# A planned transformer kernel on one core: the first unit worked off by groups of features, its first stacks loaded early, and the planner's numbers retuned

## The chip, the cores and the metric

The kernel runs on 1 core of one Trainium2 chip. The metric is the device time of one execution in microseconds (us); lower is better. Every engine (PE is the matrix engine, ACT ScalarE, DVE VectorE, POOL GpSimd, SP the engine that here only issues DMAs) works through its own instructions in the order written, and waits on semaphores for the others.

## The reference: what is computed

Eight batches of 1024 tokens with 256 features, float32, through two layers. Each layer is a transformer block with adaptive layer normalisation (shift, scale and gate from a conditioning vector `c` through `silu(c) @ wmod`):

```
h = layernorm(x) * (1 + scale1) + shift1
x = x + gate1 * attention(h)          # 16 heads of 16, causal softmax
h = layernorm(x) * (1 + scale2) + shift2
x = x + gate2 * ffn(h)
```

Layer 0 has attention with a linear bias over positions and a feed-forward part with token mixing, a sigmoid gate and a squared ReLU; layer 1 has rotary embedding on queries and keys and a linear feed-forward part whose weight is a base matrix plus a low-rank product.

## The kernel before

Work is cut into 16 **units**, one for each batch and layer, in the order (0,0), (1,0), (0,1), (2,0), (1,1) and so on, so that a batch's two layers are two units apart. A unit has these kinds of items:

- *pre*: `ln` (layer normalisation: statistics on DVE, 4 steps of a chain on DVE, 14 on POOL, then `xn` on ACT), `turned` (transposes on PE), `qk` (8 turns: w = 0 for the queries and 1 for the keys, ft = one of two groups of 128 features, tb = one of two blocks of 512 tokens), `hi` on ACT and `split` on POOL (queries and keys as a float16 pair), `parts_save` (SP writes the pairs to DRAM), `value`.
- `stack_load` (SP reads one of four groups g of 4 heads back from DRAM into `stack_q` and `stack_k`, which hold one unit). Group 0 and 1 come from features ft = 0, groups 2 and 3 from ft = 1.
- `max` (L1634): 18 steps for each group, a first pass of scores whose row maxima DVE takes (L1419, L1421); then `join`, `rows` (L1643) and four small DMAs (L1037) that put the maxima into the stack.
- `score` (L1656) with ACT's exponential (L1208), `mask` on POOL (L1087), `context` (L1675), `save` and `norm`.
- *post*: `proj`, a second `ln`, the feed-forward part and the addition to x.

The order on every engine comes from one list. `plan` (L415) is a greedy planner in Python: at each step it takes, from the queues `score`, `context`, `max`, `pre` and `post`, the item with the lowest `price`, by a model of the engines with written-down costs (`Model`), waits (`SEEN`, `DMA_NS`) and pulls (`PULL`, `AHEAD`, `PHASES`, `FEED_WAIT`). The pre and post queues are kept in order. `with_start` adds what is done once: loads, the modulations `mods` (both layers' matrices `wmod`), the low-rank product and gates `once`, and `spill`. A stack group of unit u+1 can be loaded only when unit u's scores of that group are done.

One line matters below, in `Model.other`, the cost of a step of the chain (n = 0 is the aggregation on DVE):

```
self.ready["ln"] = self.ready["factors"] = self.run(engine, begin, 75 * (item[6] - item[5]) if n == 0 else 77, 110)
```

The first matrix product of the modulations (L1540), the gates (L1548), transposes (L1690), `qk` (L1580) and `value` (L1707) are the lines of PE at the start.

## Time and profile before

| what | value |
|---|---|
| median of 3 runs | 2705.45 us (2704.71 to 2705.87) |
| the profiled execution's own time | 2702.86 us |
| its span in the trace | 2701.1 us |
| PE busy | 2432.1 us, 90% |
| DVE busy | 2127.8 us, 79% |
| ACT busy | 1701.9 us, 63% |
| POOL busy | 1025.6 us, 38% |
| mean granted clock of PE | 0.968 of full speed |

Busy time is the union of an engine's instructions. PE at 90% leaves some 269 us in which it does nothing. The 1.8 us between span and time lie outside the trace.

### The profile page before, as it was taken

Reading aid. Unit: us, or ns where it says so; the run is one execution under the profiler, and the core shown is the slowest. Engines: PE = TensorE matmul, PEld = TensorE weight load, DVE = VectorE, ACT = ScalarE, POOL = GpSimd, SP = SyncE. Lnnn points to the kernel's source line nnn. Section 1 sums busy time; section 2 is a strip of 40 time slices with the busy share of each in tenths; the row PEclk is TensorE's granted clock in tenths of the full one; section 3 lists DMA queues with packets and bytes.
Section 4 is the critical chain, followed back from the end, with each engine's and each line's share of the span. In section 5 each row is a group of like instructions: output and inputs, shape, how many; then the busy total and the mean of one; then the engine's idle time right before and its main releaser. Section 6 shows DMA issues by size and latency. Waiting matters only on the chain. (4 is left out here: it accounts for less than half of the span.)

```text
span 2701.1 us, 56435 instructions
## 1 busy us (share of the span) xinstructions
PE 2432.1 (90%) x18968; PEld 1023.9 (38%) x18968; DVE 2127.8 (79%) x6588; ACT 1701.9 (63%) x3458; POOL 1025.6 (38%) x1558
## 2 busy tenths in 40 slices
PE   7798888999999999999999999999999999898586
PEld 4323434324334343443434343343434434344223
DVE  3898738898887988879887888879888798862972
ACT  3476574576765667666676677666677666665164
POOL 4222452245332544236243453325342363326222
PEclk9999999999999999999999999999999999999798
DMA  6511134113322222322312133222223123002300
GB/s 219 166 58 35 38 109 119 47 44 103 105 81 75 79 88 89 92 72 83 116 61 83 51 102 105 83 81 72 91 88 102 60 83 109 21 31 74 97 2 16
DMA packets 142400, 218.38 MB, mean 81 GB/s; under 512 B 21190, under 2 KB 62556, under 8 KB 142052
## 3 DMA queue, kind: packets, MB, share of 16 engines
q1 hardware_dynamic: 142120, 214.77, 25.9%
q8 instruction: 160, 2.62, 0.4%
q14 instruction: 120, 0.98, 0.1%
HBM read 137.87 MB, written 77.89 MB: 80 GB/s over the span
## 5 line engine op out<-in xcount | busy, mean ns | idle before, releaser
L1208 ACT ACTIVATE probs<-big 128x512 f32<-128x512 f32 (+2 forms) x2560 | 1218.9, 573 | 457.1 <-PE big L1656 451.5
L1421 DVE CUSTOM_DVE_ANT_0 big<-big,mask 128x128 f32<-128x128 f32 (+3 forms) x2048 | 940.0, 518 | 157.3 <-PE big L1634 155.0
L1656 PE MATMUL big<-stack_q,stack_k 64*128 64x512 f16 (+3 forms) x6144 | 684.6, 330 | 69.6 <-DVE mx L1421 27.0
L1419 DVE TENSOR_REDUCE mx<-big 128x1 f32<-128x512 f32 x1024 | 644.0, 679 | 119.2 <-PE big L1634 115.1
L1675 PE MATMUL ctx_ps<-probs,v_ones 128*17 128x512 f32 (+3 forms) x6144 | 645.3, 501 | 28.2 <-POOL probs L1087 26.6
L1087 POOL TENSOR_SCALAR_AFFINE_SELECT probs<-probs 128x512 f32<-128x512 f32 x512 | 332.5, 660 | 591.1 <-ACT probs L1208 590.9
L1634 PE MATMUL big<-stack_k,stack_q 64*128 64x512 f16 (+3 forms) x3072 | 434.9, 332 | 74.7 <-DVE mx L1421 39.5
L1656 PEld LDWEIGHTS big<-stack_q,stack_k 64*128 64x128 f16 x6144 | 222.5, 94 | 668.9 <-issue 470.9
L1634 PEld LDWEIGHTS big<-stack_k,stack_q 64*128 64x128 f16 x3072 | 136.3, 94 | 410.8 <-issue 254.3
L1421 DVE DVE_READ_ACCUMULATOR2_ANT mx<- 128x1 f32 x2048 | 282.8, 138 | 0.0
L1580 PE MATMUL big<-hT,w_qkv 128*128 128x512 f32 x512 | 266.4, 629 | 1.4 <-DVE mx L1421 0.5
L1180 POOL TENSOR_TENSOR region<-region 128x512 f16<-128x512 f32 x128 | 146.1, 1158 | 214.0 <-ACT region L1250 214.0
L1118 POOL TENSOR_TENSOR ctx_n<-ctx_b 128x256 f32<-128x256 f32 x128 | 83.0, 649 | 374.1 <-DVE ctx_b L1454 374.1
L1675 PEld LDWEIGHTS ctx_ps<-probs,v_ones 128*17 128x17 f32 x6144 | 109.8, 96 | 266.5 <-issue 190.2
L1257 ACT ACTIVATE xn<-x_res,nmr,rstd 128x256 f32<-128x256 f32 x256 | 129.5, 587 | 88.9 <-POOL nmr L1097 88.9
L1234 ACT ACTIVATE region<-big 128x512 f32<-128x512 f32 x128 | 76.5, 597 | 163.8 <-PE big L1580 163.8
L1451 DVE STREAM_TRANSPOSE ctx_b<-ctx_u 128x512 f32<-128x512 f32 x128 | 90.0, 703 | 77.9 <-ACT ctx_u L1218 77.9
L1707 PE MATMUL big<-w_qkv,hT 128*128 128x128 f32 x1024 | 143.0, 287 | 0.6 <-ACT region L1234 0.2
L1707 PEld LDWEIGHTS big<-w_qkv,hT 128*128 128x128 f32 x1024 | 123.6, 193 | 26.0 <-issue 15.8
L1591 PE MATMUL big<-w_out,ctxT 128*128 128x256 f32 x512 | 117.6, 386 | 8.5 <-DVE ctxT L1457 4.6
L1591 PE MATMUL big<-w_ffn,region 128*128 128x256 f32 x512 | 120.6, 390 | 3.9 <-DVE region L1485 3.7
L1690 PE MATMUL big<-ident,xn 128*128 128x128 f32 x512 | 78.6, 311 | 44.7 <-ACT xn L1257 42.9
(94 smaller groups left out, 1923.3 us busy)
## 6 DMA issues: line engine op xcount, KB each, us to landing
image<-region SPq DMA_DIRECT2D x192, 256.0 KB
stack_q<-image SPq DMA_DIRECT2D x64, 512.0 KB, 3.7
stack_k<-image SPq DMA_DIRECT2D x64, 512.0 KB, 4.5
lo_dram<-region SPq DMA_DIRECT2D x64, 256.0 KB
w_qkv<-wqkv SPq DMA_DIRECT2D x16, 768.0 KB, 4.9
x_res<-x SPq DMA_DIRECT2D x32, 256.0 KB, 2.9
stack_q<-lo_dram SPq DMA_DIRECT2D x128, 64.0 KB, 3.8
stack_k<-lo_dram SPq DMA_DIRECT2D x128, 64.0 KB, 4.5
```

The costliest lines, as they stand in the source:

```text
L1087: g.affine_select(out=diag, in_=diag, compare_op=ALU.is_ge, fill=0.0, base=0, pattern=[[0, GH], [1, P]], channel_multiplier=-1).then_inc(m ...
L1180: g.tensor_tensor(lo, own, hi, ALU.subtract).then_inc(split_done, 1)
L1208: s.activation(probs[:, n % HELD, heads, q0:], big[:, at.slot(turn), 0:len(pairs) * width] .rearrange("p (h q) -> p h q", h=len(pairs)), A ...
L1257: ins = s.activation(xn[:, t, :], x_res[:, batch % STREAMS, t, :], ACT.Identity, scale=rstd[:, t:t + 1], bias=nmr[:, t:t + 1])
L1419: last = v.reduce_max(to, held, AX)
L1421: last = v.tensor_tensor_reduce(out=held, in0=held, in1=mask[:, BANK - width:], scale=1.0, scalar=3.0 * NEG, op0=ALU.add, op1=ALU.max, acc ...
L1580: last = te.matmul(big[:, at.slot(), :], w[:, c, ft * P:(ft + 1) * P], rhs[:, c, tb * BANK:(tb + 1) * BANK], start=(c == 0), stop=(c == FC ...
L1591: last = te.matmul(big[:, at.slot(), t * D:(t + 1) * D], lhs[:, c, (n * 2 + t) * P:(n * 2 + t + 1) * P], w[:, c, :], start=(c == 0), stop= ...
L1634: last = te.matmul(big[:, at.max_bank(parity)[0], col:col + width], stack_q[rows, 0, g * PAIR_N + pair, qt * P:(qt + 1) * P], stack_k[rows ...
L1656: last = te.matmul(big[:, at.slot(at.turn() + parity), j * width:(j + 1) * width], stack_k[rows, c, g * PAIR_N + pair, kt * P:(kt + 1) * P ...
L1675: last = te.matmul(ctx_ps[32 * h:32 * h + DH + 1, q0:], v_ones[:, (2 * unit + g // 2) % V_HALVES, kt, (g % 2) * GH + h, :], probs[:, n % H ...
L1707: last = te.matmul(big[:, at.slot(), j * P:(j + 1) * P], h_all[:, c, t * P:(t + 1) * P], w_qkv[:, 2, c, half * P:(half + 1) * P], start=(c ...
```

## The change

It has four parts. (1) Unit 0's pre part gets an order of its own, `first_sequence`: both halves of the layer normalisation ahead of the first transposes, then queries and keys of ft = 0 for both blocks, their save, then ft = 1 and the values, and their save. (2) The saves of ft = 0 have a semaphore of their own, `early_saved`; stack groups 0 and 1 are loaded behind them, ahead of the saves of ft = 1, and groups 2 and 3 after those. No `max` is planned before the last `value` of unit 0. (3) Of the work done once, the modulations of layer 0 are cut in two (the half for the first normalisation stays ahead, the other half and the gates go behind `qk`), one wmod matrix gets another place in SBUF, two of the four loads of fixed rows and the x of batch 2 go behind the weights, and the memset of `stack_k` is cut in four. (4) The planner's numbers: a chain step on POOL is 200 ns and 85 ns to be seen, where it was 77 and 110; `SEEN`, `DMA_NS`, `FEED_WAIT` and `PHASES` have other values.

```diff
+def first_sequence():
+
+    first, second = layernorm_items(0, 0, 0, NT // 2), layernorm_items(0, 0, NT // 2, NT)
+    out = first + second[:-NT // 2] + turned(0, 0, 0) + second[-NT // 2:]
+    for ft in range(FC):
+        for tb in range(2):
+            out += turned(0, 0, 1) if (ft, tb) == (0, 1) else []
+            out += [(kind, 0, w, ft, tb) for w in range(2) for kind in ("qk", "hi", "split")]
+        out += [("value", 0, half, n) for half in range(2) for n in range(2)] if ft else []
+        out += [("parts_save", 0, w, ft) for w in range(2)]
+    return out + [("pre_loads", 1)]
...
-SEEN, DMA_NS = 326.2839, 466.9094
+SEEN, DMA_NS = 315.9617, 421.9575
...
+FIRST_FEED, FEED_WAIT = {"max": 216.0, "score": 430.0}, 160.9967
...
-                self.ready["ln"] = self.ready["factors"] = self.run(engine, begin, 75 * (item[6] - item[5]) if n == 0 else 77, 110)
+                self.ready["ln"] = self.ready["factors"] = self.run(engine, begin, 75 * (item[6] - item[5]) if n == 0 else 77 if engine == "DVE" else 200,
+                                                                              110 if engine == "DVE" else 85)
...
+        if kind == "parts_save" and item[2:] == (0, 1):
+            return ("stack_load", 0, 1) not in seen
...
-                if ("stack", *item[1:3]) not in model.ready:
+                if ("stack", *item[1:3]) not in model.ready or ("value", 0, 1, 1) not in seen:
...
-    after = {("stack_load", 0, 0): [("spill", 0), ("post_loads", 0)]}
+    after = {("pre_loads", 1): [("spill", 0), ("post_loads", 0), ("fixed_rows", 1)] + [("x_load", 2, n) for n in range(4)]}
...
+                    if not unit:
+                        sp.wait_ge(early_saved, 16 * SAVE_DMAS)
+                    if unit or g >= NG // 2:
+                        sp.wait_ge(parts_saved, at.now("parts_save", 0, 16 * SAVE_DMAS))
...
-            g.memset(stack_k[:, 1], 0.0).then_inc(stacks_clear, 1)
+            for g_ in range(NG):
+                g.memset(stack_k[:, 1, g_ * PAIR_N:(g_ + 1) * PAIR_N], 0.0).then_inc(stacks_clear, 1)
```

The planner's order changes with it everywhere. First, PE behind the last values of unit 0 (L1707 before, L1753 in the change; the row of `ident,xn` is unit 1's 16 transposes, `hT,w_qkv` is unit 1's `qk`, `stack_k,stack_q` is `max`). Before:

```order
L1707 MATMUL big<-w_qkv,hT 128x128 x16
L1690 MATMUL big<-ident,xn 128x128 x16
L1580 MATMUL big<-hT,w_qkv 128x512 x2
L1634 MATMUL big<-stack_k,stack_q 128x128 x2
L1634 MATMUL big<-stack_k,stack_q 128x384 x2
L1634 MATMUL big<-stack_k,stack_q 128x256 x4
L1580 MATMUL big<-hT,w_qkv 128x512 x2
```

PE at the same place in the change:

```order
L1753 MATMUL big<-w_qkv,hT 128x128 x16
L1736 MATMUL big<-ident,xn 128x128 x16
L1680 MATMUL big<-stack_k,stack_q 128x128 x2
L1680 MATMUL big<-stack_k,stack_q 128x384 x2
L1680 MATMUL big<-stack_k,stack_q 128x256 x4
L1680 MATMUL big<-stack_k,stack_q 128x512 x4
L1680 MATMUL big<-stack_k,stack_q 128x128 x2
```

The first `max` still stands behind unit 1's transposes; the `qk` that stood between is now behind the whole of group 0.

Second, PE in the change where the first `score` stands (`stack_q,stack_k`, L1702; it was L1656). Before, 33 steps of `max`, 8 turns of `qk` and 3 of `value` stand ahead of it; here 44, 7 and none beyond those of unit 0:

```order
L1627 MATMUL big<-hT,w_qkv 128x512
L1680 MATMUL big<-stack_k,stack_q 128x512 x4
L1627 MATMUL big<-hT,w_qkv 128x512
L1680 MATMUL big<-stack_k,stack_q 128x512 x2
L1627 MATMUL big<-hT,w_qkv 128x512
L1702 MATMUL big<-stack_q,stack_k 128x512 x8
```

What moved is the first `score` against `max`: 11 steps further back.

Third, SP from unit 0's first save on, in the change (`image<-region` and `lo_dram<-region` are saves; before, all four pairs of them stood ahead of the first load of `stack_q`):

```order
L1044 DMA image<-region 8x16x1024 [waits split_done]
L1044 DMA image<-region 8x16x1024 x2
L1046 DMA lo_dram<-region 128x1024
L1044 DMA image<-region 8x16x1024 [waits split_done]
L1044 DMA image<-region 8x16x1024 x2
L1046 DMA lo_dram<-region 128x1024
L1061 DMA stack_q<-image 128x2x1024 [waits early_saved,rows_in]
...
L1044 DMA image<-region 8x16x1024 [waits split_done,stacked_1,stacked_0]
```

The saves of ft = 1 now wait until the first two stack groups have landed.

## Rows read from the trace of the kernel before

**Rows 1.** The page: the head, busy time and instructions of PE and DVE.

```profile
PE 2432.1 (90%) x18968; PEld 1023.9 (38%) x18968; DVE 2127.8 (79%) x6588; ACT 1701.9 (63%) x3458; POOL 1025.6 (38%) x1558
```

**Rows 2.** Stretches: length, busy us by engine (x count), PEclk, DMA share, GB/s.

```profile
80.00:104.00 24.00, 16.74 (x68) 4.68 (x67) 23.67 (x82) 6.13 (x10) 14.80 (x13) 0.98 0.77 215
121.60:238.50 116.90, 106.39 (x1026) 32.88 (x1025) 111.09 (x359) 86.23 (x182) 27.14 (x44) 1.00 0.20 61
238.50:420.00 181.50, 156.20 (x1103) 68.02 (x1103) 106.33 (x316) 113.88 (x227) 82.10 (x121) 0.96 0.22 66
2540.00:2580.00 40.00, 26.35 (x195) 8.49 (x195) 36.57 (x123) 14.12 (x32) 8.75 (x12) 0.66 0.15 44
```

**Rows 3.** PE's timeline: start, length, what, idle before and its releaser.

```profile
12.15 6.97 PE L1540 MATMUL big<-ctx_b,region 128*128 128x8 f32 x32 [12.15 <-DMA region<-wmod]
19.05 3.58 PE L1548 MATMUL ctx_ps<-region,ctx_b 128*8 128x256 f32 x8
22.56 1.97 PE L1690 MATMUL big<-ident,xn 128*128 128x128 f32 x8
...
59.16 3.84 PE L1707 MATMUL big<-w_qkv,hT 128*128 128x128 f32 x32
72.04 3.67 PE L1690 MATMUL big<-ident,xn 128*128 128x128 f32 x16 [9.04 <-ACT xn L1257]
...
77.73 0.61 PE L1634 MATMUL big<-stack_k,stack_q 64*128 64x128 f16 x8
...
121.63 1.12 PE L1656 MATMUL big<-stack_q,stack_k 64*128 64x512 f16 x8
...
238.46 7.14 PE L1591 MATMUL big<-w_out,ctxT 128*128 128x256 f32 x32 [0.78 <-DVE ctxT L1457]
```

**Rows 4.** PE's waits from 600 to 2400 us: us, times, longest.

```profile
PE big L1656 <- DVE mx L1421: 18.4, 38, 1.9
...
PE big L1690 <- ACT xn L1257: 6.5, 6, 1.8
```

**Rows 5.** ACT's timeline: the first normalised tiles.

```profile
17.08 2.07 ACT L1257 ACTIVATE xn<-x_res,nmr,rstd 128x256 f32<-128x256 f32 x4 [13.42 <-POOL nmr L1097]
```

**Rows 6.** SP's timeline: the first save, the first stack load.

```profile
40.16 2.03 SPq L1008 DMA_DIRECT2D image<-region  x3
...
65.76 0.37 SPq L1023 DMA_DIRECT2D stack_q<-image  x1
```

**Rows 7.** DVE's timeline: the first step of `max`, and the first `join`.

```profile
78.19 0.30 DVE L1421 CUSTOM_DVE_ANT_0 big<-big,mask 128x128 f32<-128x128 f32 x1 [13.20 <-PE big L1634]
...
102.39 0.19 DVE L1430 TENSOR_TENSOR mxc<-mx 128x32 f32<-128x32 f32 x1 [0.33 <-DVE mx L1421]
```

**Rows 8.** The page's costliest groups: busy us, mean ns | idle before.

```profile
L1656 PE MATMUL big<-stack_q,stack_k 64*128 64x512 f16 (+3 forms) x6144 | 684.6, 330 | 69.6 <-DVE mx L1421 27.0
L1675 PE MATMUL ctx_ps<-probs,v_ones 128*17 128x512 f32 (+3 forms) x6144 | 645.3, 501 | 28.2 <-POOL probs L1087 26.6
L1634 PE MATMUL big<-stack_k,stack_q 64*128 64x512 f16 (+3 forms) x3072 | 434.9, 332 | 74.7 <-DVE mx L1421 39.5
```

**Rows 9.** PE's timeline: a `max` visit of four matmuls, one of two.

```profile
1007.09 0.61 PE L1634 MATMUL big<-stack_k,stack_q 64*128 64x512 f16 x4
1007.62 0.84 PE L1675 MATMUL ctx_ps<-probs,v_ones 128*17 128x384 f32 x8
...
1024.20 0.39 PE L1634 MATMUL big<-stack_k,stack_q 64*128 64x512 f16 x2 [0.37 <-DVE mx L1421]
1024.52 1.05 PE L1675 MATMUL ctx_ps<-probs,v_ones 128*17 128x512 f32 x8
```

**Rows 10.** Timelines near the end: saves, first load, DVE's additions; the last unit's transposes.

```profile
2478.27 2.27 SPq L1008 DMA_DIRECT2D image<-region  x3
...
2494.78 0.39 SPq L1023 DMA_DIRECT2D stack_q<-image  x1
...
2494.78 0.69 DVE L1464 TENSOR_TENSOR x_res<-x_res,big 128x512 f32<-128x512 f32 x1 [3.24 <-PE big L1591]
...
2425.66 3.68 PE L1690 MATMUL big<-ident,xn 128*128 128x128 f32 x16 [5.50 <-ACT xn L1257]
```

More of the change, by code:

```diff
@@ L159, with save_of, saved_early @@
 QK_LAGS = (0.0, 0.7758, 0.9862, 2.3391, 5.9576)
+def first_sequence():
[8 more added lines that the diff above has]
+    return out + [("pre_loads", 1)]
+def save_of(unit, g):
+    return [("parts_save", unit, w, *((g // 2,) if unit == 0 else ())) for w in range(2)]
+def saved_early(item):
+    return item[0] == "parts_save" and item[3:] == (0,)
 def pre_sequence(unit):
     layer = UNITS[unit][1]
+    if unit == 0:
+        return first_sequence()
     out = normed_and_turned(unit, 0)
@@ L292, in other_needs @@
         if kind == "parts_save":
-            return max(self.at(("split", *item[1:], ft, tb)) for ft in range(FC) for tb in range(2)), "SP"
+            return max(self.at(("split", *item[1:3], ft, tb)) for ft in item[3:] or range(FC) for tb in range(2)), "SP"
         if kind == "ln":
@@ L350, in other @@
             self.ready[kind, item[1]] = self.moved(self.run("SP", begin, 450), 768, 0.180)
+            if item[1] == 1:
+                self.ready["post_loads", 0] = self.moved(self.run("SP", begin, 2600), 2400, 0.180)
         elif kind == "parts_save":
-            self.ready[kind, item[1], item[2]] = self.moved(self.run("SP", begin, 3600), 2048, 0.180)
+            self.ready[item] = self.moved(self.run("SP", begin, 3600), 1024 if item[3:] else 2048, 0.180)
     def bank(self, end):
@@ L473, in barred @@
         if kind in ("scale", "bias"):
-            return (("post_loads", unit) if unit else ("stack_load", 0, 0)) not in seen or open_("pre", unit, "ln")
+            return (("post_loads", unit) if unit else ("pre_loads", 1)) not in seen or open_("pre", unit, "ln")
         return False
@@ L509, in follow @@
                 u, g = loads[0]
-                saved = model.at(("parts_save", u, 0), ("parts_save", u, 1))
-                if ("parts_save", u, 1) not in seen or (u and ("last", u - 1, g) not in seen) \
-                        or saved > max(now, model.free["SP"]) + EASE:
+                saved = model.at(*save_of(u, g))
+                if save_of(u, g)[1] not in seen or (u and ("last", u - 1, g) not in seen) \
+                        or (u, g // 2) != (0, 0) and saved > max(now, model.free["SP"]) + EASE:
                     break
@@ L656, in events @@
         e["turn"] = 2 if kind == "score" else 1
+    if kind == "parts_save" and item[3:]:
+        del e[kind]
+        if item[2]:
+            e["early_save" if saved_early(item) else kind] = 1
     if kind == "max":
@@ L1001, in step @@
                     own = qk_place(layer, w)[1]
-                    for ft in range(FC):
+                    saved = early_saved if saved_early(item) else parts_saved
+                    for ft in item[3:] or range(FC):
                         heads, half = slice(ft * HH, (ft + 1) * HH), slice(0, DH)
@@ L1532, in _, with modulations @@
             pe.wait_ge(consts_set, 3)
-            def modulations(l):
-                for k, part in enumerate((0, 3, 1, 4)):
+            def modulations(l, which):
+                for k in which:
+                    part = (0, 3, 1, 4)[k]
                     for fc in range(FC):
@@ L1557, in once @@
                     gates_of(1, small[0:B, 1, :])
-                    modulations(1).then_inc(once_mm, 1)
+                    modulations(1, range(4)).then_inc(once_mm, 1)
                     pe.wait_ge(once_v, 1)
```

62 lines of the change are left out of this document (34 added, 28 removed).

## The prediction

> **What bounds the kernel now.** I read the page first. PE is busy 2432 of 2701 us and DVE 2128 [rows 1], so on the average PE is the bound, with 269 us of idle time in which any gain must lie, beside what PE's own work costs. Then the busy time by stretches [rows 2]. It shows that the average hides three regimes. From 80 to 104 us DVE is busy 23.67 of 24.00 us: the row maxima of unit 0 fill it, and PE waits. From 121.6 to 238.5 us DVE still has 111.1 of 116.9 and PE 106.4. After 238.5 both fall (156.2 and 106.3 of 181.5): unit 2 needs unit 0's result, and the work that may be put between runs short. The timeline of PE [rows 3] dates the marks that matter here: the last value at 59.16, unit 1's transposes at 72.04, the first `max` at 77.73, the first `score` at 121.63, unit 0's first `proj` at 238.46. The list of PE's waits in the middle of the run [rows 4] shows which waits the retuned planner could remove: on DVE's maxima 18.4 us in one of its groups, on `xn` only 6.5 us in 1800.
>
> **The start of unit 0.** Before, the first transposes begin at 22.56 [rows 3], though their tiles are ready at 17.08 + 2.07 = 19.15 [rows 5]: PE still works on the modulations and gates. In the change half of the modulations (6.97 / 2 = 3.5 us) and the gates (3.58) stand behind `qk`, so the transposes can begin at about 19.2, 3.4 us earlier, and the second half's chain no longer waits on DVE behind the modulations, which may double it to 6.8. The moved work comes back later: 7.1 us at the clock it had, 3.5 if it runs at twice that. So the last value of unit 0 moves by between -3.3 and +3.7 us. I take -1.3, as PE is in steady work by then. Unit 1's statistics, chain and `xn` hang on DVE's `once` steps, which move with it; so its transposes begin at about 70.7 where they began at 72.04.
>
> **The early stacks.** The four saves and their landing took from 40.16 to 65.76, 25.6 us [rows 6]. Two of them take 12.8, and the first begins some 6 us earlier, when ft = 0 is done: about 34 + 13 = 47, and two stack groups have landed before 60. That is far ahead of before. But in the new order the first `max` stands on PE behind unit 1's 16 transposes, and these wait for `xn`, not for a stack. The early load therefore gives nothing of its own. What the order gives is that no `qk` turn stands between: before, 72.04 + 3.67 = 75.7 to 77.73, 2.0 us. DVE's first step moves from 78.19 [rows 7] to 78.2 - 1.3 - 2.0 = 74.9. Groups 2 and 3 come late (their saves wait for the first two stacks, their loads stand behind spill, weights, tails and x), at 95 to 100 by the same rates, and are needed after 36 steps of `max`, at about 123: hidden; without that cover each us late is lost on DVE.
>
> **The first scores.** A group of 18 steps took DVE 102.39 - 78.19 = 24.2 us [rows 7], 1.345 each. Before, 33 steps stand ahead of the first `score`: 44.4 us, and it began 43.4 after DVE's first step. In the change there are 44: 74.9 + 59.2 - 1.0 + 0.5 for the second `rows` = 133.6, where it was 121.63, **+12.0**. For PE this is a hole: in it stand 44 `max` and 7 `qk`, and nothing else. A cost for the clock comes on top. Where PE had as little to do, from 2540 to 2580, the granted clock was 0.66 and DVE was busy 91% against 99% from 80 to 104 [rows 2]; carried over 59 us that is at most 4.6 us, and 0 if the clock stays at 0.98; I take 2. So the first `score` comes 14 us late. The Trainium skill (TensorE: Matmul & The Clock Gate, "What's actually happening") says that the slow clock is the default and activity releases it; the low clock in that row agrees, and by the rule the whole hole could run at 1.2 GHz, which would make the term the 4.6 us above.
>
> From there to the first `proj` the same 86 scores have to be done. An item costs PE, from the busy time [rows 8] over 1280 scores, 768 contexts and 1152 `max` steps of the plan, 0.53, 0.84 and 0.38 us; a value turn 3.84 / 2 = 1.9 [rows 3], a `qk` turn 2.0. Into this stretch come 3 values, 1 `qk` and 1 context (8.5 us), out of it go 8 `max` (3.0): 106.4 + 5.5 = 111.9 us of PE's work. DVE's falls by 8 x 1.345 to 100. So PE is the bound, and the stretch takes 111.9 to 122.4 (with all the idle time it had), against 116.9. I take 4 us of idle: 115.9, -1. First `proj` of unit 0: **+13 us**, at about 251. Bounds +9.5 to +22. Nothing absorbs it: at `proj` both orders have done the same (86 scores), and unit 2 hangs on it.
>
> **Units 1 and 2.** PE idles 25 us between 238.5 and 420 [rows 2]. With the chain on POOL planned at its real length less of it is spent on `xn`; I take -3. Changes between the three kinds of tile on PE also fall: over the whole plan from 2128 to 2046, 33 of them in units 1 and 2 and 51 in units 5 to 12. A visit of its own costs 0.11 us: a `max` visit of four matmuls takes 1007.62 - 1007.09 = 0.53, one of two 0.32 [rows 9], so the second pair costs 0.21. That is -3 here (not all on the path): **-6** in all, between 0 and -10.
>
> **The steady middle.** 51 x 0.11 = -5.6, and of the 6.5 us of waits for `xn` [rows 4] I take 2: **-7.6**. The other waits depend on how the orders mesh. The work between a group's last `max` and its `rows`, and between a diagonal score and its context, is spread much as before, so I take 0, with 15 us either way (of 107 us of idle in that stretch a seventh).
>
> **The end.** Unit 15's stacks are loaded at 2494.78, after saves that began at 2478.27 [rows 10] and took as long. In the change these saves stand 5 scores and 3 contexts further ahead: 2.7 + 2.5 = 5.2 us gained. But `proj` of unit 14 is now mixed with the first `max`, so DVE's four additions of 0.69 fall into the stretch that DVE bounds: +2.8. Unit 15's transposes waited 5.50 us for `xn` [rows 10]; its chain begins with 5 more `max` at hand: -3. **-5.4**, between -9 and +4.
>
> **Sum.** +13 - 6 - 7.6 - 5.4 = -6.0. On the profiled execution's 2702.86 that is 2696.9; this lay 2.6 below the median, so against the runs 2699.5. I say 2698.
>
> **The rivals.**
> *The start is lost and not bought back.* The place is the stretch from the first `max` to the first `proj`. If the hole costs the +13 to +17, and the middle gives only its fewer changes (and these partly under waits, -3), the sum is +7 to +14: 2710 to 2719. For it: +13 comes from counted items and measured steps, the gains mostly from small terms. It decides once the later terms give less than 8 us. Against: the end's term has its own rows.
> *The middle meshes better.* The retuned pulls may also cut waits on DVE (18.4 us in one group alone [rows 4]) and on masks. 12 us off 107 gives 2686; with a PE-bound stretch after the hole as tight as its floor, 2680. For it: more PE work is left over in each unit, since `max` runs less far ahead. Against: the spacing of items shows no such thing.
> *The change does nothing.* The early stacks are hidden behind `xn`, and plans trade waits one for one: 2703 to 2708.
>
> **How the numbers follow.** The sum as worked out, 2690 to 2703: 0.38. Better mesh, 2675 to 2690: 0.24. Nothing, 2703 to 2710: 0.14. Loss, over 2710: 0.24. A measurement tells 0.2%, 5.4 us, so faster is under 2700: 0.24 and two thirds of 0.38, 0.48; slower 0.24; same 0.28. The range leaves out about 0.1 at either end: 2681 to 2715. The sum's own range is 2690 to 2703.
>
> **What the changed profile would show.** Unit 1's transposes at 70 to 71 with a wait on `xn`, the first `max` right behind them near 74.4; PE idle about 27 us and a lower granted clock from there to the first `score` near 134; first `proj` near 251; idle time between 600 and 2400 of about 107 us; the load of unit 15's first stack about 5 us sooner after its scores. A first `score` before 128, or a middle that is 15 us shorter or longer, would make the forecast wrong.

## The result and the profile after

The changed kernel takes **2728.73 us** (median of 4 runs, 2726.71 to 2735.23) where the kernel before took 2705.66 (4 runs beside them, 2704.71 to 2706.28). The ratio is 1.0086, 95% interval 1.0074 to 1.0098: 23 us slower. 2698 was predicted, faster by 7. The profiled execution has a span of 2727.1 us and a granted clock of 0.968, as before. On another chip the same kernel gave 2728.88 (5 runs).

The page of the changed kernel, PE's line, answers to [rows 1]:

```profile
PE 2425.3 (89%) x18968; PEld 1025.8 (38%) x18968; DVE 2128.9 (78%) x6590; ACT 1699.4 (62%) x3458; POOL 1028.0 (38%) x1561
```

PE is 6.8 us less busy over the run, near the 8.6 that was forecast for fewer changes of tile form; whether it is that is asked further down. But it is idle for 2727.1 - 2425.3 = 301.8 us where it was idle for 269.0. All of the loss is idle time, and more than all.

The windows of the changed kernel, with the columns of [rows 2] (the second and third rows are the stretches from the first `score` to the first `proj` and from there to 420):

```profile
80.00:104.00 24.00, 12.74 (x47) 3.39 (x45) 23.93 (x84) 0.00 (x0) 0.00 (x0) 0.50 0.82 258
...
136.40:254.00 117.60, 109.81 (x1068) 39.67 (x1067) 102.16 (x327) 89.06 (x188) 30.05 (x46) 1.00 0.27 80
254.00:420.00 166.00, 139.99 (x996) 63.89 (x998) 94.44 (x265) 104.92 (x208) 76.49 (x113) 0.95 0.18 57
2540.00:2580.00 40.00, 27.64 (x165) 13.84 (x169) 39.63 (x141) 12.35 (x24) 10.38 (x22) 0.79 0.05 15
```

From 80 to 104 us the hole is there that the prediction described: PE busy 12.74 of 24 us where it was 16.74, ACT not once, DVE busy 23.93 of 24, the clock granted at 0.50. PE's timeline of the changed kernel gives the marks that answer to [rows 3]:

```profile
12.00 3.56 PE L1585 MATMUL big<-ctx_b,probs 128*128 128x8 f32 x16 [12.00 <-DMA probs<-wmod]
...
19.18 1.11 PE L1736 MATMUL big<-ident,xn 128*128 128x128 f32 x4 [3.62 <-ACT xn L1297]
...
71.53 3.68 PE L1736 MATMUL big<-ident,xn 128*128 128x128 f32 x16 [10.41 <-ACT xn L1297]
75.14 1.46 PE L1680 MATMUL big<-stack_k,stack_q 64*128 64x128 f16 x10
...
124.87 0.40 PE L1689 MATMUL big<-ident,mxc 128*32 128x128 f32 x1 [4.34 <-DVE mxc L1473]
...
136.45 0.61 PE L1702 MATMUL big<-stack_q,stack_k 64*128 64x512 f16 x4
...
253.99 2.18 PE L1638 MATMUL big<-w_out,ctxT 128*128 128x256 f32 x9 [0.55 <-issue]
```

DVE's timeline in the hole: the first step of `max`, the `join` behind 18 steps, and the first step behind 36:

```profile
75.82 0.30 DVE L1464 CUSTOM_DVE_ANT_0 big<-big,mask 128x128 f32<-128x128 f32 x1 [11.65 <-PE big L1680]
...
99.73 0.19 DVE L1473 TENSOR_TENSOR mxc<-mx 128x32 f32<-128x32 f32 x1
...
127.58 0.30 DVE L1464 CUSTOM_DVE_ANT_0 big<-big,mask 128x128 f32<-128x128 f32 x1 [1.69 <-PE big L1680]
```

The first `max` is 2.6 us earlier than before, the first `score` 14.8 later, the first `proj` 15.5 later. SP's timeline, for [rows 6]: first save, first stack load, the save of ft = 1, the load of group 2:

```profile
36.39 2.02 SPq L1044 DMA_DIRECT2D image<-region  x3
...
50.14 0.38 SPq L1061 DMA_DIRECT2D stack_q<-image  x1
...
61.20 1.88 SPq L1044 DMA_DIRECT2D image<-region  x3
...
85.53 1.63 SPq L1061 DMA_DIRECT2D stack_q<-image  x1
```

The first stack load is issued 15.6 us earlier than before and 25 us ahead of its first user. PE's waits of the changed kernel from 600 to 2400 us answer to [rows 4]:

```profile
PE big L1680 <- DVE mx L1464: 21.6, 49, 2.3
PE big L1702 <- ACT probs L1247: 19.0, 51, 0.8
PE big L1702 <- DVE mx L1464: 15.2, 30, 1.7
PE ctx_ps L1721 <- POOL probs L1126: 11.6, 11, 1.6
PE big L1680 <- DVE mx L1462: 11.1, 21, 1.0
PE big L1680 <- ACT probs L1247: 9.5, 38, 1.8
PE big L1638 <- DVE region L1529: 8.5, 5, 2.8
```

and these rows of the same view of the kernel before, which [rows 4] leaves out:

```profile
PE ctx_ps L1675 <- POOL probs L1087: 16.4, 17, 2.2
PE big L1634 <- DVE mx L1421: 13.4, 47, 1.1
...
PE big L1656 <- ACT probs L1208: 9.1, 17, 0.7
...
PE big L1634 <- ACT probs L1208: 6.1, 20, 0.6
```

The waits for `xn` (6.5) are gone from these rows; 0.2 are left. In their place the `max` matmuls (L1680) wait 21.6 us for the maxima of L1464 where they waited 13.4 (then L1421), scores and `max` together wait 28.5 us for ACT where it was 15.2, and `proj`'s line waits 8.5 on `region` where it waited 0.5. Some waits fell: scores for L1464 from 18.4 to 15.2, contexts for POOL from 16.4 to 11.6. In all PE is idle 131.2 us of this window where it was idle 107.1.

To date a loss I read the last `score` of every unit off PE's timeline (unit u's is the matmul of L1702 with number 384(u + 1); the last line gives PE's last matmul). The first column is in us from the start; the others say how much later each kernel is (all traces are laid on each other at the first modulation, which moves them by up to 0.9 us). The column "again" is a second trace of the changed kernel, on another chip. The kernels of the last five columns are told of below.

```
 last score   before   changed   again   e7     e10    e17    e12     e8
 unit 0        228.5    +16.2    +16.8  +16.1   +2.1   +1.5    0.0   +0.9
 unit 1        417.4    +11.8    +11.9  +16.2   +2.3   +3.6   +1.9   +1.4
 unit 2        606.5    +14.1    +12.6  +17.7   +1.9   +4.3   +3.7   +1.6
 unit 3        752.5     +8.0     +6.4  +17.4   +1.6   -2.0   +3.6   +1.6
 unit 4        923.4    +18.9    +17.3  +18.0   +2.3   +8.9   +3.3   +1.4
 unit 5       1067.0     +9.4     +7.8  +18.1   +2.4   -0.6   +3.3   +1.4
 unit 7       1381.9    +13.5    +11.9  +18.1   +2.5   +7.3   +0.6   +1.0
 unit 9       1694.8    +18.8    +17.1  +18.2   +2.5  +15.0   +7.0   +2.8
 unit 11      2009.2    +21.4    +19.7  +18.7   +3.0  +18.7  +10.8   +1.4
 unit 12      2179.8    +32.2    +28.6  +17.5   +2.9  +26.3  +18.5   +1.5
 unit 13      2315.3    +39.4    +34.6  +18.3   +2.9  +32.9  +24.3   +3.8
 unit 15      2668.1    +24.5    +20.0  +18.8   +0.1  +18.4  +21.3  -11.1
 last matmul  2697.3    +26.1    +21.3  +19.2   +0.4  +19.7  +21.9  -10.6
```

So the changed kernel has three parts: 16 us lost by the first scores, 30 lost from unit 5 to unit 13 (27 in the second trace), 13 won at the end. Two cautions. Single traces differ: e8 and e12 have the order of before up to unit 13 and unit 5, and still stand off by up to 3.8 us there; the two traces of the changed kernel come to differ by 4.8. And the marks are not of equal work. At the last `score` of unit 5 the changed kernel has issued 76 matmuls of unit 6's `max` where the kernel before has issued 92, at that of unit 4 it is 90 against 92. So unit 5 flatters it: from unit 4 to unit 12 (82 against 92) it loses 13 us.

### The profile page after: what moved, and what is told of

Read it like the earlier page. It is cut to its first block and busy times, and to the rows that moved or that the text cites. A ratio compares the mean times of both kernels' runs of the same rounds, so it can differ in the third digit from the quotient of the medians.

```text
span 2727.1 us, 56456 instructions
## 1 busy us (share of the span) xinstructions
PE 2425.3 (89%) x18968; PEld 1025.8 (38%) x18968; DVE 2128.9 (78%) x6590; ACT 1699.4 (62%) x3458; POOL 1028.0 (38%) x1561
## 5 line engine op out<-in xcount | busy, mean ns | idle before, releaser
L1464 DVE CUSTOM_DVE_ANT_0 big<-big,mask 128x128 f32<-128x128 f32 (+3 forms) x2048 | 939.5, 520 | 205.3 <-PE big L1680 201.7
L1702 PE MATMUL big<-stack_q,stack_k 64*128 64x512 f16 (+3 forms) x6144 | 676.9, 327 | 68.7 <-ACT probs L1247 26.5
L1721 PE MATMUL ctx_ps<-probs,v_ones 128*17 128x512 f32 (+3 forms) x6144 | 638.1, 496 | 30.2 <-POOL probs L1126 21.5
L1680 PE MATMUL big<-stack_k,stack_q 64*128 64x512 f16 (+3 forms) x3072 | 445.4, 335 | 108.5 <-DVE mx L1464 49.5
L1702 PEld LDWEIGHTS big<-stack_q,stack_k 64*128 64x128 f16 x6144 | 223.2, 94 | 635.7 <-issue 444.6
L1680 PEld LDWEIGHTS big<-stack_k,stack_q 64*128 64x128 f16 x3072 | 139.2, 94 | 455.5 <-issue 231.5
L1464 DVE DVE_READ_ACCUMULATOR2_ANT mx<- 128x1 f32 x2048 | 285.0, 139 | 0.1
L1753 PE MATMUL big<-w_qkv,hT 128*128 128x128 f32 x1024 | 139.5, 286 | 0.2 <-DVE mx L1464 0.2
L1638 PE MATMUL big<-w_out,ctxT 128*128 128x256 f32 x512 | 123.7, 400 | 10.6 <-issue 5.3
L1753 PEld LDWEIGHTS big<-w_qkv,hT 128*128 128x128 f32 x1024 | 123.1, 194 | 23.3 <-issue 17.0
L1304 ACT ACTIVATE v_ones<-big 128x512 f32<-128x512 f32 x64 | 38.3, 598 | 142.2 <-PE big L1753 142.1
```

The costliest lines, as they stand in the source:

```text
L1464: last = v.tensor_tensor_reduce(out=held, in0=held, in1=mask[:, BANK - width:], scale=1.0, scalar=3.0 * NEG, op0=ALU.add, op1=ALU.max, acc ...
L1638: last = te.matmul(big[:, at.slot(), t * D:(t + 1) * D], lhs[:, c, (n * 2 + t) * P:(n * 2 + t + 1) * P], w[:, c, :], start=(c == 0), stop= ...
L1680: last = te.matmul(big[:, at.max_bank(parity)[0], col:col + width], stack_q[rows, 0, g * PAIR_N + pair, qt * P:(qt + 1) * P], stack_k[rows ...
L1702: last = te.matmul(big[:, at.slot(at.turn() + parity), j * width:(j + 1) * width], stack_k[rows, c, g * PAIR_N + pair, kt * P:(kt + 1) * P ...
L1721: last = te.matmul(ctx_ps[32 * h:32 * h + DH + 1, q0:], v_ones[:, (2 * unit + g // 2) % V_HALVES, kt, (g % 2) * GH + h, :], probs[:, n % H ...
L1753: last = te.matmul(big[:, at.slot(), j * P:(j + 1) * P], h_all[:, c, t * P:(t + 1) * P], w_qkv[:, 2, c, half * P:(half + 1) * P], start=(c ...
```

## The experiments

**Start, chain and numbers apart.** Taken roughly, the changed kernel is a new start (parts 1 to 3 of the change, which stay together here), a new cost of the chain on POOL, and new numbers (both in part 4). Each of these four kernels has some of them.

e2, the kernel before with the new numbers:

```diff
-SEEN, DMA_NS = 326.2839, 466.9094
+SEEN, DMA_NS = 315.9617, 421.9575
...
-FIRST_FEED, FEED_WAIT = {"max": 216.0, "score": 430.0}, 300.0000
+FIRST_FEED, FEED_WAIT = {"max": 216.0, "score": 430.0}, 160.9967
```

(and the new `PHASES`.) 

> Before, with only the new SEEN, DMA_NS, FEED_WAIT and PHASES. Start as before. If these numbers spoil the middle: 10 to 20 us over before, by a drift of 3 to 5 us for each pair of units. If the chain cost does: within 5 us of before.

Measured: 2728.92, ratio 1.0085 (1.0068 to 1.0102): 24 us over before, more than either case had.

e3, the kernel before with the chain's cost alone:

```diff
-... 77, 110)
+... 77 if engine == "DVE" else 200, 110 if engine == "DVE" else 85)
```

> Before, with only the chain step on POOL planned at 200 and 85 ns. The plan has 2046 changes of tile kind instead of 2128, as few as the changed kernel. If fewer changes and an honest chain are worth what the prediction gave them: 5 to 10 us under before. If the chain cost is what spoils the middle: 10 to 20 us over before, with the waits for xn gone and those on DVE and ACT grown.

Measured: **2781.54**, ratio 1.0283 (1.0268 to 1.0298). It has as many changes of tile form as the changed kernel, 2046, and is 53 us slower than that. Both expected ranges are missed: 10 to 20 us was the worse one, 76 came.

e4, the changed kernel with the chain's cost and all the numbers of before:

```diff
-SEEN, DMA_NS = 315.9617, 421.9575
+SEEN, DMA_NS = 326.2839, 466.9094
...
-... 77 if engine == "DVE" else 200, 110 if engine == "DVE" else 85)
+... 77, 110)
```

> The new start, with the chain cost and all planner numbers of before. Theory 1 (the loss has two separate parts: the hole ahead of the first score, and a middle that the new chain cost and numbers spoil): first proj of unit 0 about 15 us late as in the changed kernel, no drift behind it, so 5 to 15 us over before. Theory 2 (a late start tips the greedy order of the whole run): the middle drifts here too, 20 us or more over before.

Measured: **2781.85**, ratio 1.0282 (1.0267 to 1.0298). Its start is that of the changed kernel (last `score` of unit 0 at +16.0), and from unit 1 to 5 it falls back by 36 us more. That is theory 2's case, and more than its 20 us.

e5, the kernel before with the chain's cost and the new numbers:

```diff
-SEEN, DMA_NS = 326.2839, 466.9094
+SEEN, DMA_NS = 315.9617, 421.9575
...
-... 77, 110)
+... 77 if engine == "DVE" else 200, 110 if engine == "DVE" else 85)
```

> Chain cost and new numbers on the start of before. If the parts add up, the changed kernel less the 10 to 12 us that unit 1's last score is late: 2714 to 2720. If start and numbers only go wrong together: near before, 2700 to 2708.

Measured: 2717.04, ratio 1.0045 (1.003 to 1.006): inside the range of "if the parts add up". It adds up in this one place, the start against all the rest; the sums that follow do not add.

Over the kernel before, in us: start alone +77, chain alone +76, numbers alone +24, chain and numbers +12, all three +23. The parts do not add (chain and numbers would give 100, the start 12 or 77), and none of them is faster. Each part alone lets the planner write out a new order of 7286 items, and the order is what is timed. So to learn what a part costs, the order has to be held still.

**Orders cut and joined.** In the next kernels the order is a table. `ordered` gives the planner's items in that order, and `replay` plays them through the model, for it is the model that hands out the banks of PSUM. In the lines below `old` and `new` are the orders before and after, and `then(a, b)` is `a`, followed by what is not yet in it, in the order of `b`.

```diff
-PLAN = plan(MODEL)
+PLANNED = plan(MODEL)
+PLAN = ordered(PLANNED)
+MODEL = replay(PLAN)
```

e6, the new program and its start, then the old order:

```diff
-order = new
+order = then(new up to the first max, old)
```

> The changed program with its new start (feature groups, early saves and stack loads, mask fill in pieces), but from the first `max` on in the order of the kernel before, word for word: 33 `max` steps before the first `score`, not 44. Theory 1 (the late first `score` and the drift behind it are made by the order alone): first `max` near 75 us as in the changed kernel, first `score` at 119 to 122, and the whole at 2700 to 2707. Theory 2 (the new start costs by its own work: loads that share the queues, DVE operations beside the fill, a lower clock): first `score` near 130 or later and 2715 to 2720, although the order is the old one.

Measured: 2711.52 (8 runs), ratio 1.0021 (1.0011 to 1.0031). The time lies between the theories; the first `score` comes at 131.4, as theory 2 had it. Its PE timeline shows why:

```profile
72.72 3.38 PE L1971 MATMUL big<-ident,xn 128*128 128x128 f32 x16 [8.82 <-ACT xn L1532]
83.36 3.75 PE L1862 MATMUL big<-hT,w_qkv 128*128 128x512 f32 x4 [7.26 <-DMA w_qkv<-wqkv]
87.05 1.03 PE L1915 MATMUL big<-stack_k,stack_q 64*128 64x128 f16 x8
```

In the old order a `qk` of unit 1 stands ahead of the first `max`, and in the new program its weights land late, since SP issues their load behind the four saves (at 73.76). PE waits 7.26 us for them with the stacks long there. The line numbers are higher by the table of the order.

e7, the new order up to the first `proj`, the old one behind it:

```diff
-order = new
+order = then(new up to the first proj of unit 0, old)
```

> The changed kernel's start and its order up to the first `proj` of unit 0, and from there the order of the kernel before. Theory 1 (what is lost before the first `score` is lost for good, and the middle's own order adds the rest): the 12 to 16 us of the start stay and nothing is added, 2717 to 2721. Theory 2 (the changed middle is what repairs part of the lost start, as the last scores of units 1 to 4 suggest, and without it the loss grows): 2725 or more. Theory 3 (a middle that runs in the old order takes up a late start, because its engines wait anyway): under 2710.

Measured: 2722.23, ratio 1.0058 (1.0043 to 1.0073). That is 1.2 us beyond theory 1's range, and outside the other two. The column e7 above is the plainest of the study: +16.1 at unit 0 and +18.8 at unit 15. What is lost ahead of the first scores is not taken up anywhere in 2400 us of the old order.

e8, the old program and order, but the new order at the end:

```diff
-order = old
+order = then(old up to the last score of unit 13, new)
```

> The kernel before, start and all, up to the last `score` of unit 13, and what is left from there in the changed kernel's order. In the changed kernel the distance to before shrinks from 39 us at that point to 26 at the end. Theory 1 (the order of the last two units is better by itself): 13 us come off, 2690 to 2695. Theory 2 (the distance shrinks since work that had been put off in the middle of the changed order was done by then, or since other work had been done ahead): nothing comes off, 2703 to 2710.

Measured: **2691.80**, ratio 0.9948 (0.9934 to 0.9963): theory 1, and 14 us faster than the kernel before. The windows of before, then of e8, from 2400 to 2545:

```profile
2400.00:2545.00 145.00, 111.98 (x762) 51.69 (x760) 76.76 (x218) 70.60 (x143) 59.50 (x84) 0.87 0.30 91
```

```profile
2400.00:2545.00 145.00, 116.86 (x848) 52.04 (x840) 94.39 (x275) 78.54 (x159) 61.89 (x89) 0.92 0.28 84
```

DVE does 17.6 us more in the stretch. It is the row maxima of the last unit (118 matmuls of `max` on PE there, before 82): its first `max`, before and in e8, on PE's timelines:

```profile
2501.82 0.83 PE L1634 MATMUL big<-stack_k,stack_q 64*128 64x128 f16 x10 [1.33 <-DMA stack_k<-lo_dram]
```

```profile
2421.75 0.67 PE L1756 MATMUL big<-ident,xn 128*128 128x128 f32 x4 [0.20 <-ACT xn L1323]
...
2490.82 1.46 PE L1700 MATMUL big<-stack_k,stack_q 64*128 64x128 f16 x10 [5.07 <-DMA stack_k<-lo_dram]
```

11.0 us earlier, and the 5.50 us wait of unit 15's transposes for `xn` [rows 10] is 0.20. SP's first load of that unit's stacks in e8, which stood at 2494.78 [rows 10]:

```profile
2483.53 0.38 SPq L1089 DMA_DIRECT2D stack_q<-image  x1
```

e9, the kernel before with 2 ns on one number:

```diff
-SEEN, DMA_NS = 326.2839, 466.9094
+SEEN, DMA_NS = 328.2839, 466.9094
```

> The kernel before with one number of the planner moved by next to nothing, 2 ns in 326 (the time after which an engine is taken to see another's result). 1448 of the 7286 places of the order change, all behind place 492; it has 2105 changes of tile form for 2127. Theory 1 (the numbers of the kernel before were chosen for this one order, and any other order of the same planner is worse): 2715 to 2740, with the first 150 us as before. Theory 2 (the planner gives orders of equal worth when its numbers move a little, and what the change cost comes from its parts): 2700 to 2710.

Measured: **2720.37**, ratio 1.0055 (1.0038 to 1.0072). 2 ns in a planner's assumption, which say nothing of the chip, cost 14.4 us: theory 1.

e10, as e6 with six `max` ahead of unit 1's first `qk`:

```diff
-order = then(new up to the first max, old)
+order = then(new up to the first max + old's first 6 max, old)
```

> As the kernel with the new start and the old order, but the first 6 `max` steps stand ahead of unit 1's first projection, since in that kernel the first `max` came only at 87.5 us, behind a projection that waited to 83.4 for layer 1's weights. Still 33 `max` steps before the first `score`. Theory 1 (the new start is not slower in itself; what it lost in that kernel was this wait): first `max` near 75 us, first `score` at 119 to 122, and 2700 to 2707 in all. Theory 2 (the new start only moves the wait, since layer 1's weights come later in it): first `score` at 126 or later, and 2709 to 2713.

Measured: 2704.20 (10 runs), ratio 0.9998 (0.9989 to 1.0008). Its PE timeline, and its window from 80 to 104:

```profile
75.69 0.50 PE L1915 MATMUL big<-stack_k,stack_q 64*128 64x128 f16 x6
...
80.99 7.60 PE L1862 MATMUL big<-hT,w_qkv 128*128 128x512 f32 x12 [0.27 <-DMA w_qkv<-wqkv]
...
124.39 0.90 PE L1937 MATMUL big<-stack_q,stack_k 64*128 64x512 f16 x6
```

```profile
80.00:104.00 24.00, 19.64 (x64) 6.58 (x64) 19.28 (x59) 7.36 (x12) 14.42 (x13) 0.89 0.82 260
```

The time is as theory 1 has it. The mark is not: the first `score` comes at 124.4, 2 us beyond the upper bound, since DVE has only 19.28 us of work in these 24 where it had 23.67 [rows 2]. That is my own edit: the `qk` that the old order strings between the six moved `max` now stand in one row of twelve matmuls, and DVE has nothing to do for 4.54 us of them. Even so the new start costs nothing in front of the old order.

e11, as e10 with e8's end:

```diff
-order = then(new up to the first max + old's first 6 max, old)
+order = then(then(that, old) up to the last score of unit 13, new)
```

> The kernel of the run before this one, and from the last `score` of unit 13 on the changed kernel's order, which took 14.2 us off the kernel before. If what the stages lose and win adds up, it is 14 below the run before this one: 2686 to 2693. If the joins cost, or if the gain at the end belonged to one order ahead of it, 2695 to 2705.

Measured: 2694.15, ratio 0.9959 (0.9944 to 0.9974). It lies between the two ranges, 1.2 us over the first one's end. The gain over e10 is 10.0 us where e8 had 14.2; with 4 runs here and spreads of 4 and 8 us in the two kernels, these are hardly told apart.

e12, the changed order in the middle alone:

```diff
-order = old
+order = then(then(old up to the last score of unit 5, new) up to the last score of unit 12, old)
```

> The kernel before with the changed kernel's order in its middle alone: from the last `score` of unit 5 to that of unit 12; the rest as before. It has 2083 changes of tile form for 2127. In that stretch the changed kernel fell back by 22.9 us (9.2 to 32.1). Theory 1 (the order of the stretch makes it by itself, whatever came ahead): the last `score` of unit 12 is 18 to 26 us later than before, and the whole is 2722 to 2732. Theory 2 (the drift is an after-effect of the late start): 2703 to 2709. The prediction's own claim (fewer tile changes, the rest even) would give 2699 to 2702.

Measured: **2725.73**, ratio 1.008 (1.0065 to 1.0095). Theory 1: the middle by itself, behind an untouched start, costs 20 us. PE's waits there, before (1067 to 2180 us), five rows of thirteen, and e12 (1067 to 2202), six of thirteen:

```profile
PE big L1656 <- DVE mx L1421: 12.9, 26, 1.9
PE ctx_ps L1675 <- POOL probs L1087: 11.0, 10, 2.2
PE big L1634 <- DVE mx L1421: 6.5, 27, 0.4
PE big L1656 <- ACT probs L1208: 6.3, 12, 0.7
...
PE big L1634 <- DVE mx L1419: 3.1, 10, 0.6
```

```profile
PE big L1787 <- ACT probs L1339: 12.0, 30, 0.8
PE big L1765 <- DVE mx L1552: 11.4, 26, 2.2
PE ctx_ps L1806 <- POOL probs L1218: 9.6, 9, 1.6
PE big L1787 <- DVE mx L1552: 9.2, 10, 1.7
PE big L1765 <- DVE mx L1550: 7.9, 16, 0.9
...
PE big L1722 <- DVE region L1616: 4.5, 4, 1.7
```

At the last `score` of unit 12 e12 is 18.5 us late, of which 3.3 stood there at unit 5 already, under before's order. Between these two marks PE is idle 80.5 us where it was idle 63.2, and busy 2.1 us less. The thirteen rows sum to 57.0 before and to 71.9 in e12. The matmuls of `max` (L1634, now L1765) wait 19.3 us for DVE instead of 9.6, the scores for DVE 10.7 instead of 14.3; the scores wait 12.0 us for ACT instead of 6.3; `proj`'s line waits 4.5 on `region` for 0.2, and 4.0 in which the profile shows no wait are new. No engine got more work. Why just these waits grew was not tested: that `max` matmuls stand closer together than DVE empties their banks would explain the largest part of it.

e13, units 2 and 3 by e2's order, and e8's end:

```diff
-order = then(old up to the last score of unit 13, new)
+order = old to unit 1, e2's to unit 3, old to unit 13, then new
```

> The kernel before and its start, with units 2 and 3 in the order of the kernel that had the new numbers alone (where they took 8.4 us less, from last `score` to last `score`), and with the changed kernel's order from the last `score` of unit 13. If stages add up, 2691.8 - 8.4 = 2683, so 2681 to 2686. If the 8 us were only borrowed (other work put off, to be done in unit 4), 2690 to 2694.

Measured: 2705.66 (10 runs), ratio 1.0001 (0.9992 to 1.0011): 14 us worse than e8, and outside both ranges. At the last `score` of unit 3 it is 5.0 us ahead of before, at that of unit 5 14.9 behind. Unit 3's first `proj` comes 14.7 us later than before, although its last `score` was early: the lead was borrowed. What had been put off can be counted in the traces. At the last `score` of unit 3, before has issued 92 matmuls of unit 4's `max`, e13 only 72; at the first `proj` both have issued 112. The contexts left over are the same (32 matmuls). So 20 more matmuls of `max`, 7 or 8 steps, stand ahead of that `proj`; at 1.345 us a step on DVE [rows 7] I estimate 10 of the nearly 20 us from them. The rest is open.

**What puts the first score late.** The planner's model sends every transfer through one queue. The change adds 2400 KB to it (`post_loads` 0, behind `pre_loads` 1), and the 16 KB of the first `rows` stand behind them. Without that one entry the planner puts 36 `max` ahead of the first `score`, not 44.

e14, that entry out, for the order up to the first `proj`:

```diff
-order = new
+order = then(new without the 2400 KB, up to the first proj of unit 0, new)
```

> The changed kernel, with its order up to the first `proj` of unit 0 from a planner whose model doesn't put the 2400 KB of `post_loads` 0 into its one queue of transfers; from there the changed kernel's own order. 36 `max` steps stand before the first `score`, not 44. Theory 1 (this entry is what puts the first `score` late, and the late start is worth its 11 us in the changed kernel too): first `score` at 75.8 + 36 x 1.38 = 125.5 us (the changed kernel has 44 steps from 75.8 to 136.5, 1.38 each), between 122 and 128, and 2715 to 2720 in all. Theory 2 (the middle loses what it loses whatever the start gives): 2725 to 2731.

Measured: 2721.43, ratio 1.0057 (1.0041 to 1.0074). The cut fell between the two halves of unit 0's first output projection with a `rows` turn in between, so part of what e14 computes is wrong. Its time counts for little by itself; the join is one place earlier in e16.

> As the run whose model leaves out the 2400 KB, with the join one item earlier, ahead of the first half of unit 0's first output projection and not between its two halves. In that run the first `score` came at 120.9 us (15.5 earlier than in the changed kernel), the last `score` of unit 0 11.3 us earlier than in the changed kernel, and the whole 7.3 us. If the fault didn't touch the time, this gives 2719 to 2723 again, so that of 11 us won at the start 7 are left at the end; if it did and the start's whole worth comes through, 2715 to 2718.

Measured: 2728.49 (2721.23 to 2731.57), ratio 1.0073 (1.0053 to 1.0093). The median is outside both ranges of its expectation, and 0.2 us from the changed kernel's. The first `score` comes at 120.9 in e14 and 122.5 in e16 (laid on the changed kernel's trace), 14 to 15.5 us earlier than in the changed kernel, which shows the cause of its lateness. But the last `score` of unit 0 is only 9 to 11 earlier, and the whole 0 to 7. Theory 1 had the mark nearly right (122 to 128), its price was not.

e15, a first `score` earlier than in any other:

```diff
-order = then(then(new up to the first max + old's first 6 max, old) up to the last score of unit 13, new)
+order = then(then(new with rows outside the model's queue, up to the last score of unit 0, old) up to unit 13's, new)
```

> The new start, then up to the last `score` of unit 0 the order of a planner whose model lets the 16 KB row transfers pass the queue of large ones: 24 `max` steps before the first `score`. Then the order of the kernel before to the last `score` of unit 13, then the changed kernel's. Against it stands the kernel that was made alike with 33 steps, 2694.2. Theory 1 (ScalarE idles until the first `score`, so an early one is worth something): first `score` at 107 to 112, and 2684 to 2690. Theory 2 (VectorE is busy without a break from the first `max` to 240 us, so what comes first there changes nothing): 2692 to 2697, with the last `score` of unit 0 within 2 us of the kernel before's.

Measured: 2693.11, ratio 0.9955 (0.994 to 0.997); e11 is 2694.15, with its first `score` at 122.7. That is theory 2's time. Its PE timeline and its window to 240:

```profile
109.69 1.23 PE L1916 MATMUL big<-stack_q,stack_k 64*128 64x512 f16 x8
```

```profile
121.00:240.00 119.00, 113.27 (x1028) 38.72 (x1031) 111.73 (x363) 85.04 (x175) 33.44 (x47) 1.00 0.29 88
```

The first `score` is 12 us ahead of before, the last of unit 0 is 4.6 behind (theory 2 had within 2), and the time is e11's. With DVE busy 111.7 and PE 113.3 of 119 us, there is little idle time that an early `score` could fill.

e17, the old order up to the first `proj`, then the new:

```diff
-order = new
+order = then(e10's order up to the first proj of unit 0, new)
```

> The changed program in the old order (first 6 `max` steps first) up to unit 0's first output projection, then the changed kernel's order to the end. In front of the old order this start is worth 18 us more than the changed one (2722.2 against 2704.2). Theory 1 (stages add): 2728.7 - 18 = 2711, so 2707 to 2715. Theory 2 (the changed rest had been made for a state in which more `max` steps are done; from another state it loses what the start wins): 2720 to 2730.

Measured: 2723.50 (5 runs), ratio 1.0069 (1.0057 to 1.0082): theory 2's range. Beside it on the same chip the changed kernel once more:

> The changed kernel as it is, on the same chip as the run before this one: 2725 to 2732 by every theory.

Measured: 2728.88, ratio 1.0094 (1.0079 to 1.0109).

In one table, us over the kernel before, all in the new program and with its new start ("old order to proj" is e10's: the new order up to the first `max`, six `max`, then the old order):

```
                      rest in the old order    rest in the new order
 old order to proj      e10   -1                 e17  +19
 new order to proj      e7   +16                 changed kernel +24
```

## Why the prediction was wrong, by its own steps

**The step that failed is the steady middle.** It gave -7.6 us: 5.6 for fewer changes of tile form, 2 for `xn`, and 0 for all other waits, "with 15 us either way". From the last `score` of unit 5 to that of unit 13 the changed kernel loses 30 us (27 in its second trace). e17, with the same order behind an early first `score`, loses 33.5 there, and the new order between units 5 and 12 alone, behind an untouched start (e12), makes the whole run 20 us slower. So it is not an after-effect of the late start. The term that I set to nothing is the one that mattered: the waits on DVE and ACT (PE's idle time from 600 to 2400 us went from 107.1 to 131.2). The reason I gave, that the items are spread much as before, was a view of the order, and the order does not tell whether DVE empties a bank in time.

Of the two terms that I had worked out, the waits for `xn` did go. The 5.6 for changes of tile form is not to be seen in its place: between units 5 and 12 the changed kernel's PE is busy 1052.9 us where it was 1049.6 (with 31 matmuls more), and in e12, with 44 changes fewer, 1047.5, 2.1 less. That PE is 6.8 us less busy over the whole run comes from elsewhere (the changed kernel, from unit 13 on: 299.8 for 303.3; from the first `proj` to unit 5: 746.2 for 756.4, with 61 matmuls fewer). Nor does the number of changes tell a time: 2046 of them go with 2728.7 and with 2781.5 us (e3, where PE is even busier, 2454.7 us by its page, than before).

**"The change does nothing" and the even middle rested on an unsaid base:** that an order made by slightly other numbers is as good as this one. e9 refutes it. That the numbers had been chosen for this one order would be the natural reason; it is not shown, but it fits that all five other settings tried (e2 to e5, e9) are 12 to 77 us slower.

**The start: the number was right, and in part by luck.** Transposes of unit 1 at 71.53 (70.7 predicted) behind a wait for `xn`; first `max` on DVE at 75.82 (74.9); the early stacks give nothing (25 us of slack); first `score` at 136.45 (135.6 with the clock's 2). The hole itself, from DVE's first step to the first `score`, took 60.6 us where the sum has 60.7 (59.2 - 1.0 + 0.5 and 2 for the clock), but not by its terms. The steps took no more than before (the first 18 are done in 23.9 us, before 24.2), so the 2 us for the clock are not in them; instead DVE stood idle for 2.5 us about the second `rows`, where I had 0.5. From the first `score` to the first `proj` it took 117.5 us, not 115.9: PE's work was 109.8 (111.9 predicted) and its idle time 7.8 (4). That makes +15.5 of +13, well inside +9.5 to +22. The stacks of groups 2 and 3 were loaded from 85.53, not at 95 to 100, and were hidden as I said. e6 and e10 add what I did not see: the early saves and loads stand ahead of layer 1's weights, so a `qk` of unit 1 that is placed first waits 7.26 us.

**"Nothing absorbs it" holds ahead of the old order alone.** There the changed order up to the first `proj` costs 18.0 us (e7 against e10; both have the new start). Ahead of the new order it costs 5.4 (e18 against e17), and curing the late `score` alone gives 0 to 7. The traces tell where part of the difference goes. At its first `proj` the changed kernel has issued 104 matmuls of unit 1's `max` where the kernel before has issued 94, and one context more. e17 does these items late, ahead of its `proj`: it is 14.7 us ahead of the changed kernel at the last `score` of unit 0, and 9.0 at the first `proj`, with the same work done. 8.2 are left at unit 1, 10.0 at unit 5, 6.5 at unit 13 (1.7 against the second trace). What takes up the rest is not settled; no run isolates it.

**Units 1 and 2** got -6, between 0 and -10. With the traces laid on each other, the distance fell from 15.7 at the first `proj` to 11.8 at the last `score` of unit 1, and stood at 14.1 at that of unit 2: -4 or -1.6 by the mark, inside the bounds. The reasons are not borne out. From the first `proj` to the last `score` of unit 1 PE's idle time did not fall (26.0 us, before 25.3): the waits for `xn` went from 6.3 to 4.3, and others grew. What is less is PE's work, 149.3 for 153.9, and with 34 matmuls fewer it is largely work done earlier or later. So the number is luck as far as the waits go.

**The end was mis-sized.** It got -5.4, at most -9; the order from unit 13 on is worth -14 (e8). I counted 5.2 us for earlier saves and 3 for `xn`, and took off 2.8 for DVE's additions. In e8 the load of unit 15's stacks is issued 11.2 us earlier: the second pair of saves begins 7.6 us earlier (2470.71 for 2478.27), and from there to the load it takes 12.8 us where I let it take the 16.5 of before. The `xn` wait fell by 5.3. What the additions cost no run tells.

**The clock.** I took 2 us for it and at most 4.6. The granted clock was 0.50, that is 1.2 GHz, the lower of its two levels, from 80 to 104 us, with PE busy for half of the time. DVE was still busy 23.93 of 24 us, and its first 18 steps took 23.9 us against 24.2 before at a clock of 0.98 to 1.00: it cost them nothing. At the second `rows`, where DVE stood idle, the `qk` of two matmuls (at 125.06) took 1.91 us and the next one (at 127.87) 1.13, so some 0.8 us may be the clock's. The Trainium skill (TensorE: Matmul & The Clock Gate, "What's actually happening") has the slow clock as the default that activity releases; the row agrees. That it is nearly free while PE only feeds DVE is what this trace adds.

The rival "the start is lost and not bought back", at 2710 to 2719, named the right place and the right price of the start, and still missed: it too had the middle at no less than a small gain. And one slip in the chances: 2700 lies ten thirteenths of the way from 2690 to 2703, not two thirds, so "faster" should have had 0.53 by its own rule.

## What to carry to other kernels

When a planner writes the order, a change to any of its numbers is a new order, and its worth is unknown until it is timed; here neither the count of changes nor the engines' busy time predicted it. Measure the spread first (here 2 ns cost 14 us, so "the middle stays even" deserved a range up to tens of us), and test a code change with the order held still: the new start that seemed to cost 12 us (changed kernel against e5) or 77 (e4) costs nothing in front of the old order (e10). And orders can be cut: e8 takes from the slower kernel its better end and is 14 us faster than the kernel before. Count the work done at a cut before a lead is believed: one that is only work put off (e13) is paid back.

## What the runs showed that I had not expected

- A shift of 2 ns in one planning assumption costs 14.4 us (0.55%), a more truthful cost of POOL's steps 76 us.
- A delay of 16 us at unit 0 passes through 14 units of the old order almost unchanged (+16.1 to +18.8), though PE idles 10% of the time: this idle time is tied to the order and does not take up a delay.
- An early first `score` makes no difference here (109.69 in e15 against 122.72 in e11, with 2693.11 and 2694.15 us; 121.63 before against 124.39 in e10, with 2705.32 and 2704.20). In these kernels DVE and PE are both busy for over 90% from 121 to 240 us.
- The same order joined one item later and earlier (e14, e16) gave 2719.22 to 2723.70 and 2721.23 to 2731.57 us: single kernels here spread by up to 10 us between executions (the kernel before by 8, 2701.43 to 2709.77, over all its runs), more than the 1.6 us of its first four.
